# A four-layer graph network on one core: reciprocals scattered a stage earlier, the last node block in two scatters, no rests before the last ends

## The reference

```python
# layer 0 ("powers"), four times over
y = segment_sum(weights[:, None] * y[col], row)              # row = src, col = dst
# layer 1 ("conv"): piecewise-linear basis of two edge attributes
out = segment_sum(sum_k(t[:, k, None] * (x[col] @ w[k])), row)
# layer 2 ("relate0", "relate1"): relational convolution, twice
cnt = zeros(n, 8).at[dst, edge_type].add(1.0)
norm = 1.0 / maximum(cnt[dst, edge_type], 1.0)
agg = segment_sum(msg * norm[:, None], dst) + x @ root + bias
# layer 3 ("message"): tensor product with 8 edge attributes, silu, segment_sum(m, row)
```

## Time and profile before

| | us |
|---|---|
| median of 3 runs | 18782.5 |
| lowest, highest | 18770.41, 18819.21 |
| the profiled execution | 18798.8 |
| its span, first to last instruction | 18797.0 |
| busy: TensorE, VectorE, ScalarE, GpSimd | 15061.3, 14607.7, 11866.0, 10732.2 |
| GpSimd's scatters in powers, 2912 | 3548.1 |

### The profile page before, as it was taken

The page is one execution under the profiler, slowest core; times in us unless marked ns, Lnnn a source line. Parts: engine busy times, 40 slices in busy tenths (PEclk is TensorE's granted clock), DMA queues, the critical chain, the costliest instruction groups (busy, mean ns, idle before and its releaser), DMA issues. The chain is left out here.

```text
span 18797.0 us, 353555 instructions
## 1 busy us (share of the span) xinstructions
PE 15061.3 (80%) x83251; PEld 13368.1 (71%) x83252; DVE 14607.7 (78%) x36172; ACT 11866.0 (63%) x23181; POOL 10732.2 (57%) x33516
## 2 busy tenths in 40 slices
PE   0158828887887888788699988999919999689997
PEld 0058828887887888788688885777607777489996
DVE  4845557777777777777699997999808888689997
ACT  2000027776776777677577777888718888567775
POOL 0468837775775775777477706666652243477720
PEclk9555559998998999899899998999959999899998
DMA  7611120000000000000111112222201122111111
GB/s 226 122 28 39 39 75 23 22 22 22 22 22 22 22 22 23 21 22 23 31 31 31 31 24 64 70 70 72 66 18 60 64 66 65 42 31 30 30 27 17
DMA packets 1258063, 826.18 MB, mean 44 GB/s; under 512 B 863939, under 2 KB 1202983, under 8 KB 1250343
## 3 DMA queue, kind: packets, MB, share of 16 engines
q1 hardware_dynamic: 865126, 670.89, 12.9%
q0 software_dynamic: 274432, 117.81, 3.5%
q10 hardware_dynamic: 118080, 33.61, 1.0%
HBM read 586.84 MB, written 234.66 MB: 44 GB/s over the span
## 5 line engine op out<-in xcount | busy, mean ns | idle before, releaser
L1534 PE MATMUL powers_sums<-powers_b_hot,powers_spread 128*128 128x224 f32 x26400 | 5269.3, 364 | 1047.1 <-DVE powers_b_hot L1515 1000.9
L1534 PEld LDWEIGHTS powers_sums<-powers_b_hot,powers_spread 128*128 128x128 f32 x26400 | 5160.7, 197 | 1158.0 <-issue 1114.1
L1619 POOL DMA_INDIRECT filled<-powers_by_b,powers_at_start x2912 | 3548.1, 1218 | 1918.7 <-issue 865.3
L2299 PE MATMUL relate_got<-relate_hot,relate_table 112*128 112x512 f32 (+1 forms) x10560 | 3076.9, 434 | 68.9 <-ACT relate_hot L2261 68.9
L1529 ACT ACTIVATE powers_b_hot<-powers_away,ones 128x672 f32<-128x672 f32 x2640 | 1981.8, 753 | 1600.3 <-PE powers_sums L1534 1393.6
L1523 ACT ACTIVATE powers_away<-wide,powers_minus_b 128x224 f32<-128x224 f32 x6600 | 2719.2, 472 | 117.4 <-ACT powers_minus_b L1687 37.6
L2299 PEld LDWEIGHTS relate_got<-relate_hot,relate_table 112*128 112x128 f32 x10560 | 1697.6, 191 | 1340.9 <-issue 1269.1
L1512 DVE TENSOR_TENSOR powers_spread<-powers_a_hot,powers_message 128x640 f32<-128x640 f32 x2640 | 2157.8, 817 | 233.7 <-PE powers_sums L1534 138.8
L2261 ACT ACTIVATE relate_hot<-relate_away,ones 112x1280 f32<-112x1280 bf16 x1320 | 1799.4, 1363 | 508.1 <-PE relate_got L2299 453.7
L1515 DVE TENSOR_SCALAR powers_b_hot<-wide,powers_b_val 128x224 f32<-128x224 f32 x6600 | 1940.5, 343 | 0.0
L2314 PE MATMUL relate_mixed<-relate_mix,relate_picked 128*128 128x128 f32 x13200 | 1704.2, 276 | 39.4 <-DVE relate_picked L2363 39.4
(11 more groups left out here) (473 smaller groups left out, 26115.0 us busy)
## 6 DMA issues: line engine op xcount, KB each, us to landing
relate_codes<-pair_rows SPq DMA_DIRECT2D x264, 800.0 KB
powers_given<-filled SPq DMA_DIRECT2D x528, 200.0 KB
rec<-relate_running SPq DMA_DIRECT2D x132, 400.0 KB
filled<-powers_by_b,powers_at_start POOLq DMA_INDIRECT x2912
grouped<-order_blanks POOLq DMA_DIRECT2D x20, 1320.0 KB
filled<-order_blanks SPq DMA_DIRECT2D x20, 1320.0 KB
held_recs<-grouped SPq DMA_DIRECT2D x132, 200.0 KB
conv_given<-filled SPq DMA_DIRECT2D x132, 200.0 KB
```

The costliest lines, as they stand in the source:

```text
L1534: mm = pe.matmul(gathering.sums[:, bass.ds(group * STRIDE, WINDOW)], spread[:, j].rearrange("p a d -> p (a d)"), b_hot[:, j, :], start=Fal ...
L1619: pool.indirect_dma_start(filled, bass.IndirectOffsetOnAxis(at_start[0:n, k, a, i:i + 1], 0), g.by_b[0:n, k, a * D:(a + 1) * D], None).the ...
L2299: mm = pe.matmul(got[:, n % 2, at:to], table[:, n // SLOTS % 2, half, :], flat[:, at:to], start=half == 0, stop=half == 1, skip_group_chec ...
```

## The change

1. **powers:** the last node block is not scattered as 8 times 32 rows but as 2 times 128. For that its 256 rows are also loaded in another layout (`tail`, with their places in `tail_at`), by SP: once at the start, and again behind each round's write. The rests are counted by scatters sent.
2. **conv:** when GpSimd has landed its own 91 blocks, it scatters the first 26 blocks of reciprocals (groups 0 and 1), 208 scatters with a rest before every second. SP lays the reciprocals out for it at the stage's start, as relate0 does again at its own.
3. **relate0:** the scatters of those 26 blocks are left out; their first rows are still gathered, behind one rest a block.
4. **relate0, relate1:** no rests in the last group's ends.

```diff
+EARLY_BLOCKS = 26
+CUT = B_ALL // P * P * 8
+def sends(block):
+    return 2 if block % B_BLOCKS == B_BLOCKS - 1 else 8
+def sent(blocks):
+    return sum(sends(b) for b in blocks)
@@ powers, SP
+            sp.dma_start(tail_at[:], starts[CUT:ROWS].rearrange("(s p) t -> p s t", p=P)).then_inc(starts_in, 16)
...
+            sp.dma_start(tail[:], node_rows[CUT:ROWS].rearrange("(s p) d -> p s d", p=P)).then_inc(tail_in, 16)
             with sp.Fori(0, rounds) as r:
...
+                sp.wait_ge(y_in, r * 32 + 64)
+                sp.sem_inc(tail_free, 1)
+                sp.wait_ge(blocks_ready, r * SPREAD_BLOCKS + SPREAD_BLOCKS)
+                sp.dma_start(tail[:], node_rows[CUT:ROWS].rearrange("(s p) d -> p s d", p=P)).then_inc(tail_in, 16)
@@ powers, GpSimd
+                    if block == B_BLOCKS - 1:
+                        pool.wait_ge(tail_in, r * 16 + 16)
+                        pool.sem_inc(gate, 1)
+                    for a in range(sends(block)):
+                        many = sent(range(block)) + a
+                        if many % BURST == 0 and many:
+                            rest(pool, still, rested, r * ((sent(range(SPREAD_BLOCKS)) - 1) // BURST) + many // BURST, gate)
+                        if sends(block) == 8:
+                            to, rows = at_start[:, k, a, i:i + 1], g.by_b[:, k, a * D:(a + 1) * D]
+                        else:
+                            to, rows = tail_at[:, a, i:i + 1], tail[:, a, :]
@@ expanded_sums, SP
+            if inverses is not None:
+                sp.dma_start(by_hi(inverses.rows), inverses.values[:]).then_inc(types_out, 16)
+                sp.wait_ge(types_out, 16)
+                for lanes, ks, dram in g.rows(inverses.rows, T):
+                    sp.dma_start(type_rows[lanes, ks], dram).then_inc(types_in, 16)
@@ expanded_sums, GpSimd
             landed(SPREAD_BLOCKS - 1)
+            if inverses is not None:
+                rests = rests_upto(SPREAD_BLOCKS, -1, CALM_BURST)
+                pool.wait_ge(types_in, 32)
+                pool.sem_inc(gate, 1)
+                for block in range(EARLY_BLOCKS):
+                    i, k = block // B_BLOCKS, block % B_BLOCKS
+                    n = min(P, B_ALL - k * P)
+                    for a in range(8):
+                        if (block * 8 + a) % CALM_BURST == 0 and block + a:
+                            rest(pool, still, rested, rests + rests_upto(block, a, CALM_BURST), gate)
+                        pool.indirect_dma_start(inverses.filled, bass.IndirectOffsetOnAxis(at_start[0:n, k, a, i:i + 1], 0),
+                                                type_rows[0:n, k, a * T:(a + 1) * T], None).then_inc(types_spread, 16)
+                pool.wait_ge(types_spread, 16 * 8 * EARLY_BLOCKS)
@@ relation_sums, GpSimd
-                    pool.wait_ge(spread_out[half], 16 * 8 * (block // 2 + 1))
+                    if block >= EARLY_BLOCKS:
+                        pool.wait_ge(spread_out[half], 16 * 8 * len(range(EARLY_BLOCKS + half, block + 1, 2)))
...
-                    for a in range(8):
-                        if (block * 8 + a) % CALM_BURST == 0 and block + a:
-                            rest(pool, still, rested, rests_upto(block, a, CALM_BURST), gate)
+                    for a in range(8 if block >= EARLY_BLOCKS else 0):
+                        if a % CALM_BURST == 0:
+                            rests += 1
+                            rest(pool, still, rested, rests, gate)
...
+                    if block < EARLY_BLOCKS and first_turns(block) > first_turns(block - 1):
+                        rests += 1
+                        rest(pool, still, rested, rests, gate)
...
-                    if h % CALM_BURST == 0:
+                    if h % CALM_BURST == 0 and g < GROUPS - 1:
```

More of the change, by code:

```diff
@@ L1487, in rest @@
 def rest(pool, still, rested, count, gate):
-    for k in range(RESTS):
+    for k in range(still.shape[1]):
         ins = pool.memset(still[:, k:k + 1], 0.0)
@@ L1568, in powers @@
             "mid", "ready", "taken", "gate", "last_in"))
+        tail_free = s.sem("tail_free")
         block = s.block()
@@ L1604, in landed @@
                     half = block % 2
-                    pool.wait_ge(spread_out[half], r * (16 * 8 * len(range(half, SPREAD_BLOCKS, 2))) + 16 * 8 * (block // 2 + 1))
+                    pool.wait_ge(spread_out[half], r * (16 * sent(range(half, SPREAD_BLOCKS, 2))) + 16 * sent(range(half, block + 1, 2)))
                     pool.sem_inc(blocks_ready, 1)
@@ L2547, in landed @@
                         pool.sem_inc(firsts_ready, count)
+                rests = 0
                 for block in range(SPREAD_BLOCKS):
@@ L2563, in _ @@
                 landed(SPREAD_BLOCKS - 1)
-            rests = rests_upto(SPREAD_BLOCKS, -1, CALM_BURST) if count_types else 0
+            if not count_types:
+                rests = 0
             for g in range(GROUPS):
```

21 lines of the change are left out of this document (12 added, 9 removed).

## The result

| | before | after |
|---|---|---|
| median us of the comparison | 18799.1 | 18349.6 |
| lowest, highest | 18770.4, 18819.2 | 18339.0, 18365.5 |
| span of the profiled execution | 18797.0 | 18354.9 |

A forecast was written before the change was run, and what follows sets the result against it. GpSimd's queue was taken as the bound in powers and relate0's last 400 us. 240 - 13 - 3 + 365 + 44 = 633 us off the median 18782.5 gave 18150 us, range 18095 to 18260.

The forecast's parts named there:

- Part 4: relate1: without rests the last group's gathers end sooner and all of it counts; 44 us gained (18 to 47).
- the 122 us for the last group in relate0: relate0's end: 98 gathers without a rest, at 0.95 us each and 0.30 between, take 122 us.
- rival (c): Last groups of relate0 and relate1: gathers without rests back up at 1.218 us each, both lose 26 us; 18200, chance 0.08.
- Part 1: powers: 42 scatters and 10 rests fewer a round shorten GpSimd's queue; 60 us a round, 240 for four.
- the low bound of 212: powers: least gain for four rounds, with 53 us a round; the upper bound was 261.
- the seventh block: powers: the last of a round's seven shortened blocks gives at most 2.9 us, since VectorE is late next.
- The bound for cheaper 32-row scatters: powers: at 0.87 us for each removed scatter and 0.09 more for the two kept, 53 us a round.
- Part 2: conv: 208 added scatters fit under its cover in 407 us; VectorE loses 13 us, SP's write of reciprocals costs 3.
- rival (b): conv: VectorE starves the early scatters, which outlast the stage; 18355 at chance 0.03, at the far end 18860 at 0.01.
- Part 3: relate0: without the 208 scatters GpSimd's work moves forward by 337 us and the stage ends sooner; 365 us gained.
- rival (d): relate0: GpSimd waits for each landing in the short blocks, as in part 3's low bound; 18200, chance 0.10.
- The stretch of about 60 us with GpSimd alone: Sign at relate0's end: the time when only GpSimd works falls from 400 to about 60 us.

The follow-up runs named there:

- norests_only: The kernel before with only the rests of the last group's ends left out; ratio 0.996, in two later loadings 0.9991 and 0.9987.

## Why the prediction was wrong

Some 17 of the 200 us between 18150 and 18349.6 are no part of the gain: the forecast counted from 18782.5, and beside the changed kernel the one before had 18799.1. The other 183 are missing in the gain.

**Part 4, and the end of part 3: the failed step.** "VectorE is idle for the second half of these gathers, so I take 44 us", and the 122 us for the last group in relate0. The 122 us were near: it measured 124.7 from first to last start, with 0.95 us a gather and 0.33 between in the mean. What failed is that the price was looked for on GpSimd alone; rival (c) too asked only what slows the gathers, and what they cost the other engines was no term of the sum. The evidence taken for a long unpaused run was none: the 98 gathers at L1065 have 153.8 us of idle time between them, 1.57 us each, and 124.3 of it is a wait for VectorE. In relate1 before, the arithmetic of the last pairs runs for 66 us beside these gathers. That cover was in the text ("idle for the second half"), but not what the first half is worth. Held up, its last repair comes 60 us behind the last gather in relate0, and the stage ends 58 us behind GpSimd's addition. In relate1 the forecast gain of 44 became a loss of 17, in relate0 365 became 318. The Trainium skill ("SBUF — State Buffer", "Who interferes with whom") says that PE and ACT never wait on anyone. That is said of SBUF ports; if it is read as freedom from GpSimd altogether, these traces disagree for TensorE: 81 matmuls in 120 us beside unpaused gathers, 551 in 100 before.

**Part 1, powers: the mechanism right, its term mis-sized.** 170 us for 240, below the low bound of 212. Over all traces, powers as before takes 6300.8 to 6336.0 us (seven, mean 6316.3) and the changed powers 6126.4 to 6159.0 (ten, mean 6141.4): 175 less. Two quantities of the step explain it. First, the text itself said that "a good part of the removed collisions returns on the rest", and took 60 a round all the same; in fact all of them returned, and somewhat more. Counting scatters over 2 us in the two traces: before, 227 of 2912, of which 24 on the 224 scatters of the last node block; after, 228 of 2744, one of them on the tail. A round's 42 scatters at 1.218 are 51 us, but the 686 that stay became 37 ns dearer in the mean (3443.3 / 2744 = 1.255), which takes 25 back. With 42 gaps of 0.30 and ten rests at 0.88 that leaves 26 + 13 + 9 = 48, and the scatters of a round span 46 less in the mean. Second, the last pair of a round comes 82 us behind the last scatter, after 76 to 78 before. That leaves 42 a round: 46, 38, 54 and 31 by VectorE's pairs. GpSimd's third round begins 85 us earlier after its first scatter, where 120 were forecast. In the prediction's own terms: at 0.96 us for each removed scatter the sum was 56 a round, but what the scatters cost above 0.96 us grew from 188 to 202 us a round, and 56 - 14 is the 42 measured. That the seventh block gives nearly nothing, VectorE being late next, was right. The bound for cheaper 32-row scatters was added up a little high (8 x 1.17 - 2 x 1.26 + 1.26 = 8.1 for a group makes 51.5 a round and not 53), which changes nothing: before, the scatters of the last node block took 1.246 us in the mean, no less than the others' 1.216.

**Part 2: right.** Forecast 13 + 3 us lost, measured 20. The 208 scatters and their rests took 403.6 us (407 forecast) at 1.161 us each, the slowest 2.337, and were over 92 us before conv's last load, where 45 were forecast, so rival (b) was nowhere near. The 3.1 us that the prediction quoted from the Trainium skill ("SBUF — State Buffer", "A bandwidth-pool intuition that's wrong (but worth ruling out)") didn't appear on any of them.

**Part 3: right but for its last 58 us.** GpSimd's path became 374 us shorter, 365 were forecast; the short blocks did not wait for their landings as in rival (d). The stretch of about 60 us with GpSimd alone, forecast as a sign, does not occur, since the arithmetic ends behind the gathers.

## What to carry to other kernels

Pauses between GpSimd's indirect transfers may not be for GpSimd's sake. Before removing them, look at which engines have work beside that stretch and price their loss; where nobody has any, remove them. The change with the last group's rests kept for gathers 0 to 39, and dropped only after the last pair's arithmetic, had the lowest ratio here: 0.9717 against 0.9763.

And a removed transfer is worth its undisturbed time at most, not the group's mean, if that mean holds collisions that another engine's instructions cause, for these find another one. A single loading of a program on one chip can also mislead: norests_only looked harmless in all its executions there, and its relate1 took 55 us more in two later loadings on other chips.

Where a row names a releaser that was done long before, or "issue" ahead of an instruction that by the program waits for a semaphore, read the program for what it waits for, and that instruction's end and update.

## What was not expected of the hardware

- Ninety-eight indirect transfers issued one behind the other, every 1.28 us, held TensorE to about an eighth of its pace (81 matmuls in 120 us after 551 in 100) for nearly their whole length, and with it ScalarE and VectorE, which waited for its results. The semaphore of a matmul came 31.8 us behind its recorded end, in place of 0.01. With a pause of 0.88 us after every second, there was no trace of it (pairs of 33.4 us); after every fourth, pairs of 36 to 54 us.
- The effect did not depend on how many rows each transfer carried (32 or 128).
- One program, norests_only, showed it on two chips and not on a third, and on each the times of all its executions agree. Whether the chip or the loading decides isn't shown.
